# First attention: the keys of a group are loaded with its queries and ahead of them

## The chip, the cores and the metric

The program runs on one core of one Trainium2 chip. The core has TensorE (matmuls, PE in the profile), VectorE (DVE), ScalarE (ACT), GpSimd (POOL) and SyncE (SP), which here does nothing but issue DMAs; the DMAs are carried out by 16 DMA engines of the core. The metric is device time in microseconds of one execution, as a median over runs. The profile is one execution of its own.

## The reference, cut to what matters

`x` and `ctx_2048` have the shape 64 x 64 x 256. Eight blocks follow each other (four pairs of an attention and a feed-forward block), each added to `x`. The change touches the first block alone:

```
def _L0_xattn_ref(q, k, v):            # q = layernorm(x), k = v = ctx_2048
    h = 8
    qh = q.reshape(b * h, d // h, m)   # d = 64: eight channels in each head, m = 256 columns
    kh = k.reshape(b * h, d // h, -1)
    vh = v.reshape(b * h, c // h, -1)
    qk = jnp.einsum('bdm,bdn->bmn', qh, kh) * scale
    sm = jax.nn.softmax(qk, axis=-1)
    return jnp.einsum('bmn,bcn->bcm', sm, vh)
x = x + _L0_xattn_ref(_layernorm(x), ctx_2048, ctx_2048)
```

So there are 64 batches of eight heads, and for each head a 256 x 256 matrix of scores, a softmax over its rows, and a product with the values.

## The kernel before, in words

`first_attention` works through 64 **units** (one batch each, eight heads). A float is split into three bf16 parts, and a score is a product over 72 partitions (nine combinations of parts times eight channels). For that the split parts are stored in DRAM (`z_parts` for the queries, `context_parts` for the keys, lines 185 and 190) and read back spread over partitions: `Q9` (queries, `ratt_Q` in the profile) and `K9` (keys, `ratt_K`). One read serves a **group** of two units, 576 KB of queries (one DMA, line 200) and 576 KB of keys (three DMAs of 192 KB, line 209). There are four buffers of each (`BUFS`), and one semaphore for a buffer, `group_in`, counts the landings of both; TensorE waits for all 64 of a group before the first score of its first unit.

A unit passes twice over TensorE. In slot n, `score(n, h)` (line 419) makes the scores, VectorE takes the maximum of each row of scores (line 591), GpSimd splits these maxima in three bf16 parts (lines 371 to 375), TensorE turns them (`turn_max`, line 428), ScalarE copies the turned row (line 502, semaphore `row_out`), and SP writes it with two small DMAs (`bring_row`, line 216) to three further partitions of `Q9` (semaphore `row_in`). Three slots later (`LAG`), `shift_scores` (line 437) makes the scores again, now with the maxima taken off by those three partitions; it waits for `row_in` at its first head. ScalarE takes the exponential (line 509) and TensorE multiplies with the values (line 461). In the row of PE, score of unit n and shifted score of unit n - 3 take turns, head by head.

The order of each engine is written out by hand: every engine runs a loop over the slot number n, and what stands in one turn of the loop is issued in that order. SP's turn n is, in this order: for n of kind B (below) a load of `x` and of the context (lines 174 and 180); `bring_row(n - 1)`; for odd n `load_q` of the group that starts at unit n + 3; for even n `load_k` of the group that starts at unit n + 2; and then, by n modulo 4, the outputs of four finished units (lines 223, 228, 233, 238 and 240) and the stores of the split parts (lines 185 and 190). SP waits in its order, so `bring_row(n - 1)`, which waits for the row of unit n - 1, holds back all that stands behind it.

In the following a slot is named by n modulo 4: **A** is 0, **B** is 1, **C** is 2 and **D** is 3. Four slots, A to D, are a **period**. The units that open a group are those of A and of C. Before the change, the group that opens at A has its queries issued in SP's turn B and its keys in turn C, and the group that opens at C has its queries issued in turn D and its keys in turn A. SP's turn n begins when the row of unit n - 1 is out, that is late in TensorE's slot n.

`load_q` waits, besides for the stores of `z_parts`, until the last shifted scores of the unit that used the buffer before are written (`written`, four groups earlier). `load_k` had no such wait of its own, as it stood behind `load_q` of the same group.

Of the kernel before, what the change touches and what calls it, by code (L numbers as in the profile page):

```python
# [72 lines left out]
def spread(ap, dim, n):  # L73

    return ap.unsqueeze(dim).to_broadcast(list(ap.shape[:dim]) + [n] + list(ap.shape[dim:]))

def first_attention(nc, io, X, CT, ident, identb, zq, ck, o_dram, r_dram, ST, wsum):
# [3 lines left out]
    BUFS = 4  # L81
# [8 lines left out]
    with ExitStack() as ctx:  # L90
# [21 lines left out]
        veps, rstd, shift = s.sb("veps", [P, 2]), s.sb("rstd", [P, 2]), s.sb("shift", [P, 2, 2])  # L112
# [28 lines left out]
        written, exped, v_in, pv, o_out = (s.sem(x) for x in ("written", "exped", "v_in", "pv", "o_out"))  # L141
# [4 lines left out]
        def is_unit(n):  # L146
            return 0 <= n < UNITS

        def is_pair(a):
            return 0 <= a < PAIRS  # L150

        def at(n, r):

            a, left = divmod(n + LEAD - r, 4)
            return a if left == 0 and is_pair(a) else None

        job, jobs = {}, 0
# [9 lines left out]
        with nc.Block() as block:  # L167

            @block.sync
            def _(sp):  # L170
                def load_x(a):
                    if a > 1:
                        sp.wait_ge(x_in[a % 2], a // 2 * 16)
                    sp.dma_start(X[:, 2 * a:2 * a + 2, :],
                                 x_dram[2 * a:2 * a + 2].rearrange("t p d -> p t d")).then_inc(x_in[a % 2], 16)

                def load_c(a):
                    if a > 1:
                        sp.wait_ge(c_third, a - 1)
                    sp.dma_start(C[:, a % 2],  # L180
                                 c_dram[2 * a:2 * a + 2].rearrange("t p d -> p t d")).then_inc(c_in[a % 2], 16)

                def store_c(a, part):
                    sp.wait_ge((c_first, c_second, c_third)[part], a + 1)
                    sp.dma_start(ck.rearrange("r s a h u m -> s a h r (u m)")[part, a],
                                 CS[:, part].rearrange("p u m -> p (u m)")).then_inc(c_out[part], 16)

                def store_z(a, part):
                    sp.wait_ge((z_first, z_second, z_third)[part], a + 1)
                    sp.dma_start(zq.rearrange("s r a h u m -> s a h r (u m)")[part, a],  # L190
                                 ZS[:, part].rearrange("p u m -> p (u m)")).then_inc(z_out[part], 16)

                def load_q(g):
                    pair, b = g // 2, g % 2
                    for part in range(3):
                        sp.wait_ge(z_out[part], pair * 16 + 16)
                    if g >= BUFS:
                        sp.wait_ge(written, job["shift", 2 * (g - BUFS) + 1, 3] + 1)
                    q = zq.rearrange("s r a (b h) u m -> (s r) a b (h u m)", b=2)[:, pair, b, :]
                    sp.dma_start(Q9[0:R, g % BUFS].rearrange("p h u m -> p (h u m)"), spread(q, 1, 3)).then_inc(  # L200
                        group_in[g % BUFS], 16)

                def load_k(g):
                    pair, b = g // 2, g % 2
                    for part in range(3):
                        sp.wait_ge(c_out[part], pair * 16 + 16)
                    k = ck.rearrange("r s a (b h) u m -> (r s) a b (h u m)", b=2)[:, pair, b, :]
                    for part in range(3):
                        sp.dma_start(K9[24 * part:24 * part + 24, g % BUFS].rearrange("p h u m -> p (h u m)"),
                                     k).then_inc(group_in[g % BUFS], 16)  # L210

                def bring_row(n):
                    u, buf = n % 2, n // 2 % BUFS
                    sp.wait_ge(row_out, n + 1)
                    for c in range(2):
                        sp.dma_start(Q9[R:RM, buf, :, u, c * P:(c + 1) * P],
                                     rows[c * 3 * NH0:(c + 1) * 3 * NH0, u, :]).then_inc(row_in[u], 16)

                def out(a):
                    sp.wait_ge(o_out, a * 4 + 4)  # L220
                    for g in range(4):
                        to = o_dram.rearrange("a (w g) c m -> a g c w m", g=4)[a, g]
                        sp.dma_start(to, O[32 * g:32 * g + DH0 + 1, a % 2].rearrange(
                            "p w u m -> p w (u m)")).then_inc(to_dram[a % 2], 16)

                def sums_back(a):
                    sp.wait_ge(to_dram[a % 2], a // 2 * 64 + 64)
                    sp.dma_start(inv[:, a % 2], o_dram[a][:, DH0, :].rearrange(
                        "w (k m) -> w k m", k=8)).then_inc(d_in[a % 2], 16)

                def inverses_out(a):
                    sp.wait_ge(inverted, a + 1)
                    sp.dma_start(r_dram.rearrange("a w (k m) -> (a w k) m", k=8)[a * P:(a + 1) * P],
                                 inv[:, a % 2]).then_inc(r_out[a % 2], 16)

                def back(a):
                    sp.wait_ge(r_out[a % 2], a // 2 * 16 + 16)
                    sp.dma_start(den[:, a % 2].rearrange("p u m -> p (u m)"), spread(r_dram[a], 1, DH0)).then_inc(
                        o_back[a % 2], 16)
                    sp.dma_start(num[:, a % 2].rearrange("p u m -> p (u m)"), o_dram[a][:, 0:DH0, :]).then_inc(  # L240
                        o_back[a % 2], 16)

                sp.dma_start(decay[:], spread(io["L3_xattn_decay"], 0, P)).then_inc(decay_in, 16)
                for n in range(-LEAD - 3, UNITS + 11):
                    if at(n, -3) is not None:
                        load_x(at(n, -3))
                        load_c(at(n, -3))
                    if is_unit(n - 1):
                        bring_row(n - 1)
                    if n % 2 and is_unit(n + 3):  # L250
                        load_q((n + 3) // 2)
                    if n % 2 == 0 and is_unit(n + 2):
                        load_k((n + 2) // 2)
                    c = n // 4 - 2
                    if n % 4 == 0:
                        if is_pair(c - 1):
                            inverses_out(c - 1)
                        if is_pair(c):
                            out(c)
                    if n % 4 == 1 and is_pair(c):  # L260
                        sums_back(c)
                    if n % 4 == 2 and is_pair(c - 1):
                        back(c - 1)
                    for part in range(3):
                        if at(n, 3 + part) is not None:
                            store_c(at(n, 3 + part), part)
                        if at(n, 6 + part) is not None:
                            store_z(at(n, 6 + part), part)
                    if n == -LEAD + 1:
                        sp.wait_ge(ones_set, 1)  # L270
                        for buf in range(BUFS):
                            sp.dma_start(K9[R:RM, buf].rearrange("p h u m -> p (h u) m"),
                                         spread(ones[:], 1, 2 * NH0)).then_inc(ones_in, 16)
# [3264 lines left out]
```

## Time and profile before

| what | us |
| --- | --- |
| median of 3 runs | 1953.99 (1953.58 to 1956.91) |
| the profiled execution, whole | 1960.88 |
| its span in the trace | 1959.0 |
| first attention: first score to last score | 31.9 to 499.0 |

The span is the time from the first to the last instruction in the trace; about 1.9 us lie around it. The profiled execution took 6.9 us more than the median of the timed runs.
### The profile page before, as it was taken

How to read it: one execution, taken by the hardware profiler on the slowest of the kernel's cores; microseconds unless marked ns; L12 is line 12 of the kernel's file. 1: busy time of each engine (PE TensorE's matmuls, PEld its weight loads, DVE VectorE, ACT ScalarE, POOL GpSimd, SP SyncE). 2: the span in 40 equal slices, each digit the busy share in tenths (PEclk: the TensorE clock that was granted, in tenths of full speed). 3: DMA queues.
4: the chain of work that ended last, by engine and by line, in shares of the span. 5: the costliest groups of instructions: out<-in, count | busy, mean ns of one | idle time of the engine just before them, and what ended most of it. 6: DMA issues, size and time to landing. Idle time of an engine off the chain costs nothing. (4 is left out here: it accounts for less than half of the span.)

```text
span 1959.0 us, 32199 instructions
## 1 busy us (share of the span) xinstructions
PE 1359.7 (69%) x11551; PEld 857.7 (44%) x11572; DVE 1317.5 (67%) x2817; ACT 1105.8 (56%) x1568; POOL 575.1 (29%) x1047
## 2 busy tenths in 40 slices
PE   3989889899469876987435666379999546773111
PEld 1655555555257762555312333246666423442100
DVE  4777677677245534688849999536665567775896
ACT  2767676676412214677537889534444437775554
POOL 6555555553300013111013433201110111112663
PEclk9989898899779997999655667679999768777555
DMA  5565665655310003433010000011111210000111
GB/s 157 130 158 149 143 156 146 165 123 134 78 31 1 0 5 62 78 73 74 9 69 1 1 1 1 22 38 45 30 38 33 91 23 1 1 1 11 44 54 43
DMA packets 96676, 118.46 MB, mean 60 GB/s; under 512 B 29984, under 2 KB 82408, under 8 KB 91916
## 3 DMA queue, kind: packets, MB, share of 16 engines
q1 hardware_dynamic: 96524, 116.46, 24.1%
q8 instruction: 91, 1.49, 0.3%
q14 instruction: 61, 0.50, 0.1%
HBM read 80.07 MB, written 22.88 MB: 53 GB/s over the span
## 5 line engine op out<-in xcount | busy, mean ns | idle before, releaser
L591 DVE TENSOR_REDUCE ratt_nmax<-ratt_psS 128x2 f32<-128x512 f32 x512 | 321.9, 685 | 129.0 <-PE ratt_psS L419 127.4
L509 ACT ACTIVATE ratt_E<-ratt_psT 128x1024 f32<-128x1024 f32 x256 | 256.2, 1023 | 124.6 <-PE ratt_psT L437 124.2
L419 PE MATMUL ratt_psS<-ratt_K,ratt_Q 72*128 72x256 bf16 x1024 | 217.3, 299 | 54.8 <-DMA ratt_K<-context_parts 48.8
L437 PE MATMUL ratt_psT<-ratt_Q,ratt_K 75*128 75x256 bf16 x1024 | 208.5, 289 | 0.6 <-ACT ratt_E L509 0.3
L419 PEld LDWEIGHTS ratt_psS<-ratt_K,ratt_Q 72*128 72x128 bf16 x1024 | 85.7, 103 | 153.5 <-DVE ratt_nmax L591 56.7
L461 PE MATMUL ratt_psO<-ratt_E,ratt_V 128*32 128x256 f32 x2048 | 148.2, 410 | 0.7 <-ACT ratt_E L509 0.7
L437 PEld LDWEIGHTS ratt_psT<-ratt_Q,ratt_K 75*128 75x128 bf16 x1024 | 105.7, 104 | 23.3 <-issue 2.1
L3414 PE MATMUL final_psT<-final_identh,final_Z 128*128 128x128 f16 x64 | 8.3, 311 | 110.4 <-ACT final_Z L3448 110.4
L461 PEld LDWEIGHTS ratt_psO<-ratt_E,ratt_V 128*32 128x32 f32 x2048 | 55.8, 114 | 56.1 <-issue 34.5
L371 POOL TENSOR_TENSOR ratt_parts<-ratt_nmax,ratt_zero 128x16 bf16<-128x16 f32 x64 | 17.1, 268 | 214.5 <-DVE ratt_nmax L591 214.5
L906 ACT COPY sffn_XS<-sffn_psG 128x512 f32<-128x512 f32 x8 | 4.7, 585 | 124.7 <-PE sffn_psG L855 124.7
L2216 PE MATMUL nffn_psH<-nffn_W,nffn_QT 128*128 128x512 bf16 x121 | 52.9, 583 | 30.9 <-ACT nffn_H L2295 20.4
L2409 POOL TENSOR_TENSOR all_X<-all_X,satt_bo 128x1024 f32<-128x1024 f32 x8 | 18.9, 2365 | 167.4 <-DVE all_X L2474 167.4
L2770 DVE SCALAR_TENSOR_TENSOR gffn_H<-gffn_psU,gffn_uwu,gffn_S 128x512 f32<-128x512 f32 x64 | 46.1, 745 | 28.4 <-ACT gffn_S L2945 27.4
L2873 PE MATMUL gffn_psG<-gffn_WG,gffn_QT 128*128 128x512 bf16 x120 | 48.3, 487 | 22.9 <-DVE gffn_H L2770 19.5
L872 PE MATMUL sffn_psH<-sffn_XS,sffn_W 128*128 128x256 f32 x256 | 59.9, 394 | 3.8 <-ACT sffn_XS L906 3.8
L2246 PE MATMUL nffn_psO<-nffn_W,nffn_HT 128*128 128x256 bf16 x256 | 47.5, 348 | 18.7 <-DVE all_X L2135 17.4
L881 PE MATMUL sffn_psO<-sffn_W,sffn_H 128*128 128x256 f32 x256 | 57.4, 383 | 4.4 <-ACT sffn_H L916 4.4
L1282 DVE SCALAR_TENSOR_TENSOR gatt_PB<-gatt_psS,gatt_PB 128x512 f32<-128x512 f32 x64 | 41.2, 686 | 26.0 <-PE gatt_psS L1023 20.8
L3414 PEld LDWEIGHTS final_psT<-final_identh,final_Z 128*128 128x128 f16 x64 | 6.2, 141 | 114.0 <-ACT final_Z L3448 83.1
L872 PEld LDWEIGHTS sffn_psH<-sffn_XS,sffn_W 128*128 128x128 f32 x256 | 49.9, 197 | 12.7 <-issue 3.0
L2587 ACT COPY satt_AT<-satt_psF 128x256 f32<-128x256 f32 x32 | 12.0, 374 | 76.4 <-PE satt_psF L2524 76.4
(474 smaller groups left out, 3693.8 us busy)
## 6 DMA issues: line engine op xcount, KB each, us to landing
ratt_Q<-z_parts SPq DMA_DIRECT2D x32, 576.0 KB
ratt_K<-context_parts SPq DMA_DIRECT2D x96, 192.0 KB
gatt_V<-in_ctx_dram SPq DMA_DIRECT2D x16, 512.0 KB, 6.7
context_parts<-ratt_CS SPq DMA_DIRECT2D x48, 128.0 KB, 5.3
z_parts<-ratt_ZS SPq DMA_DIRECT2D x48, 128.0 KB, 5.5
head_sums<-ratt_O SPq DMA_DIRECT2D x64, 72.0 KB
all_X<-in_x_dram SPq DMA_DIRECT2D x16, 256.0 KB, 3.8
ratt_C<-in_ctx_dram SPq DMA_DIRECT2D x16, 256.0 KB, 3.9
```

Of the source, the lines that this page charges most:

```text
L419: mm = nc.tensor.matmul(psS[:, RING[h], c * D:(c + 1) * D], Q9[0:R, buf, h, n % 2, c * P:(c + 1) * P], K9[0:R, buf, h, n % 2, :], start=Tr ...
L437: mm = nc.tensor.matmul(psT[:, j % 2, e, c, :], K9[0:RM, buf, h, u, c * P:(c + 1) * P], Q9[0:RM, buf, h, u, :], start=True, stop=True)
L461: mm = nc.tensor.matmul(psO[32 * g:32 * g + 32, q, :], V9[:, m % 2, c, q * 4 + g, :], E[:, m % 2 * 2 + q, g, c, :], start=(c == 0), stop=( ...
L509: sc.activation(E[:, m % 2 * 2 + p // 2, 2 * (p % 2):2 * (p % 2) + 2], psT[:, j % 2], ACT.Exp, scale=SCALE).then_inc(exped, 1)
L591: v.tensor_reduce(nmax[:, n % 2, h, :], psS[:, RING[h]].rearrange("p (c t) -> p c t", c=2), AX.X, ALU.max, negate=True).then_inc(maxed, 1)
L872: mm = nc.tensor.matmul(psH[:, f % 2, ff, :], W1[:, k, c * P:(c + 1) * P], XS[:, k, :], start=(k == 0), stop=(k == KC - 1))
L881: mm = nc.tensor.matmul(psO[:, b, :], H[:, c, b * P:(b + 1) * P], W2[:, c, :], start=(c == 0), stop=(c == FC - 1))
L1282: v.scalar_tensor_tensor(half, heads.psS[:, r].rearrange("p (h t) -> p h t", t=L), float(DH) ** -0.5, half, ALU.mult, ALU.mult).then_inc(h ...
L2216: nc.tensor.matmul(psH[:, j % 2, cols], QT[:, g % 2, k, j * P:(j + 1) * P], W1[:, k, cols], start=(k == 0), stop=False)
L2246: mm = nc.tensor.matmul(psO[:, j % 2, 0:D], HT[:, j % 2, n, :], W2[:, n, :], start=(n == 0), stop=(n == FF // P - 1))
L2770: v.scalar_tensor_tensor(H[:, g % 2, j, h * HALF:(h + 1) * HALF], psU[:, h, :], uwu[:, g % 2, j:j + 1], S[:, h, :], ALU.mult, ALU.mult).th ...
L2873: nc.tensor.matmul(psG[:, h, :], QT[:, g % 2, k * G + j, :], WG[:, k, cols], start=(k == 0), stop=(k == KC - 1))
```

## The change

`load_k` moves one slot up: it is issued in the same odd turn as `load_q` of its group, directly in front of it and directly behind `bring_row`. As it now stands ahead of `load_q`, it gets the wait for the buffer's last reader for itself.

```
--- before.py
+++ after.py
@@ -204,6 +204,8 @@
                     pair, b = g // 2, g % 2
                     for part in range(3):
                         sp.wait_ge(c_out[part], pair * 16 + 16)
+                    if g >= BUFS:
+                        sp.wait_ge(written, job["shift", 2 * (g - BUFS) + 1, 3] + 1)
                     k = ck.rearrange("r s a (b h) u m -> (r s) a b (h u m)", b=2)[:, pair, b, :]
                     for part in range(3):
                         sp.dma_start(K9[24 * part:24 * part + 24, g % BUFS].rearrange("p h u m -> p (h u m)"),
@@ -248,9 +250,8 @@
                     if is_unit(n - 1):
                         bring_row(n - 1)
                     if n % 2 and is_unit(n + 3):
+                        load_k((n + 3) // 2)
                         load_q((n + 3) // 2)
-                    if n % 2 == 0 and is_unit(n + 2):
-                        load_k((n + 2) // 2)
                     c = n // 4 - 2
                     if n % 4 == 0:
                         if is_pair(c - 1):
```

No DMA is added or taken away, and no other engine has another instruction; the whole difference is in the order of SP's queue. The first place is SP's turns B and C in the full pipeline, before: from the loads of `x` and context that open turn B, over the row of unit A and the queries of the next A, to the row and the keys that turn C issues.

```order
L174 DMA all_X<-in_x_dram 128x2x256
L180 DMA ratt_C<-in_ctx_dram 128x2x256
L216 DMA ratt_Q<-ratt_rows 3x8x128 x2
L200 DMA ratt_Q<-z_parts 72x1x4096
L228 DMA ratt_inv<-head_sums 128x1x64
L185 DMA context_parts<-ratt_CS 16x8x512
L216 DMA ratt_Q<-ratt_rows 3x8x128 x2
L209 DMA ratt_K<-context_parts 24x4096 x3
```

The same place after (line numbers from 207 on are higher by two):

```order
L174 DMA all_X<-in_x_dram 128x2x256
L180 DMA ratt_C<-in_ctx_dram 128x2x256
L218 DMA ratt_Q<-ratt_rows 3x8x128 x2
L211 DMA ratt_K<-context_parts 24x4096 x3
L200 DMA ratt_Q<-z_parts 72x1x4096
L230 DMA ratt_inv<-head_sums 128x1x64
L185 DMA context_parts<-ratt_CS 16x8x512
L218 DMA ratt_Q<-ratt_rows 3x8x128 x2
```

What moved: the keys that turn C issued (`ratt_K` x3) now stand in turn B, in front of the queries and so also in front of the summaries' load, the context store and the row of unit B.

The second place is SP's turns D and A, before, from the row of unit C to the stores of the finished units:

```order
L216 DMA ratt_Q<-ratt_rows 3x8x128 x2
L200 DMA ratt_Q<-z_parts 72x1x4096
L185 DMA context_parts<-ratt_CS 16x8x512
L190 DMA z_parts<-ratt_ZS 16x8x512
L216 DMA ratt_Q<-ratt_rows 3x8x128 x2
L209 DMA ratt_K<-context_parts 24x4096 x3
L233 DMA inverse_sums<-ratt_inv 128x64
L223 DMA head_sums<-ratt_O 9x4x512 x4
```

And after:

```order
L218 DMA ratt_Q<-ratt_rows 3x8x128 x2
L211 DMA ratt_K<-context_parts 24x4096 x3
L200 DMA ratt_Q<-z_parts 72x1x4096
L185 DMA context_parts<-ratt_CS 16x8x512
L190 DMA z_parts<-ratt_ZS 16x8x512
L218 DMA ratt_Q<-ratt_rows 3x8x128 x2
L235 DMA inverse_sums<-ratt_inv 128x64
L225 DMA head_sums<-ratt_O 9x4x512 x4
```

What moved: the keys that turn A issued stood behind two stores and behind the row of unit D; now they stand in turn D, in front of the queries, and turn A has no large load any more.

## Rows read from the trace of the kernel before

**Rows 1.** The page: span; busy engines; three of the lines in 40 slices of 49 us

```profile
span 1959.0 us, 32199 instructions
...
PE 1359.7 (69%) x11551; PEld 857.7 (44%) x11572; DVE 1317.5 (67%) x2817; ACT 1105.8 (56%) x1568; POOL 575.1 (29%) x1047
...
PEclk9989898899779997999655667679999768777555
DMA  5565665655310003433010000011111210000111
GB/s 157 130 158 149 143 156 146 165 123 134 78 31 1 0 5 62 78 73 74 9 69 1 1 1 1 22 38 45 30 38 33 91 23 1 1 1 11 44 54 43
```

**Rows 2.** Waits of 0 to 700 us: who waited for whom, us, times, longest

```profile
PE ratt_psS L419 <- DMA ratt_K<-context_parts: 48.8, 16, 15.2
...
DVE ratt_nmax L591 <- PE ratt_psS L419: 127.4, 136, 9.7
ACT ratt_E L509 <- PE ratt_psT L437: 124.2, 174, 5.4
```

**Rows 3.** Waits of the steady stretch, 83.25 to 475.57 us

```profile
PE ratt_psS L419 <- DMA ratt_K<-context_parts: 33.2, 14, 3.5
PE ratt_psT L437 <- DMA ratt_Q<-ratt_rows: 0.2, 1, 0.2
```

**Rows 4.** Windows: steady stretch, slots, transfers, an idle stretch; columns in the first line

```profile
core 0: us, PE busy (x) PEld busy (x) DVE busy (x) ACT busy (x) POOL busy (x), PEclk, DMA share, GB/s
83.25:475.57 392.32, 355.68 (x3424) 210.65 (x3425) 284.74 (x485) 274.51 (x370) 196.92 (x460) 0.90 0.61 147
83.25:89.44 6.19, 6.12 (x65) 3.71 (x66) 4.97 (x8) 4.56 (x6) 3.30 (x6) 1.00 0.54 139
171.18:180.16 8.98, 8.95 (x66) 4.85 (x66) 5.29 (x8) 4.70 (x6) 1.11 (x2) 0.65 0.37 107
180.16:186.82 6.66, 6.59 (x73) 4.17 (x69) 5.37 (x10) 6.20 (x10) 4.05 (x8) 1.00 0.52 131
186.82:193.01 6.19, 6.12 (x69) 3.72 (x66) 5.84 (x12) 5.19 (x8) 4.40 (x12) 1.00 0.70 174
193.01:202.29 9.28, 6.19 (x70) 3.71 (x66) 5.62 (x10) 5.32 (x8) 7.11 (x16) 0.95 0.91 187
202.50:205.50 3.00, 3.00 (x16) 2.09 (x14) 2.08 (x4) 1.02 (x1) 0.45 (x1) 0.50 0.83 229
213.00:216.00 3.00, 2.93 (x34) 1.92 (x33) 2.21 (x5) 2.71 (x5) 2.14 (x2) 1.00 0.69 182
237.50:242.50 5.00, 4.93 (x49) 2.98 (x43) 3.06 (x5) 3.62 (x6) 0.99 (x5) 0.86 0.01 1
```

**Rows 5.** Timeline of TensorE: first scores of units 8, 20, 24, 54, 60; the last (start, us, idle before)

```profile
83.25 0.28 PE L419 MATMUL ratt_psS<-ratt_K,ratt_Q 72*128 72x256 bf16 x1 [0.60 <-DMA ratt_K<-context_parts]
...
171.18 0.61 PE L419 MATMUL ratt_psS<-ratt_K,ratt_Q 72*128 72x256 bf16 x2 [2.84 <-DMA ratt_K<-context_parts]
...
202.29 0.39 PE L419 MATMUL ratt_psS<-ratt_K,ratt_Q 72*128 72x256 bf16 x1 [3.02 <-DMA ratt_K<-context_parts]
...
432.46 0.28 PE L419 MATMUL ratt_psS<-ratt_K,ratt_Q 72*128 72x256 bf16 x1 [0.38 <-DMA ratt_K<-context_parts]
...
475.57 0.28 PE L419 MATMUL ratt_psS<-ratt_K,ratt_Q 72*128 72x256 bf16 x1 [0.44 <-DMA ratt_K<-context_parts]
...
498.90 0.28 PE L419 MATMUL ratt_psS<-ratt_K,ratt_Q 72*128 72x256 bf16 x1
```

**Rows 6.** Timeline of SP's queue: DMA issues, start, us for the group

```profile
190.23 0.81 SPq L200 DMA_DIRECT2D ratt_Q<-z_parts  x1
191.09 0.60 SPq L228 DMA_DIRECT2D ratt_inv<-head_sums  x1
191.73 0.60 SPq L185 DMA_DIRECT2D context_parts<-ratt_CS  x1
192.37 1.55 SPq L216 DMA_DIRECT2D ratt_Q<-ratt_rows  x2
194.04 1.20 SPq L209 DMA_DIRECT2D ratt_K<-context_parts  x3
...
210.19 1.56 SPq L216 DMA_DIRECT2D ratt_Q<-ratt_rows  x2
211.87 1.18 SPq L209 DMA_DIRECT2D ratt_K<-context_parts  x3
213.10 0.36 SPq L233 DMA_DIRECT2D inverse_sums<-ratt_inv  x1
213.50 2.83 SPq L223 DMA_DIRECT2D head_sums<-ratt_O  x4
...
220.20 1.56 SPq L216 DMA_DIRECT2D ratt_Q<-ratt_rows  x2
221.92 0.81 SPq L200 DMA_DIRECT2D ratt_Q<-z_parts  x1
```

**Rows 7.** DMA view of 190.2 to 192.4 us: size, us from issue to landing

```profile
context_parts<-ratt_CS SPq DMA_DIRECT2D x1, 128.0 KB, 5.2
ratt_inv<-head_sums SPq DMA_DIRECT2D x1, 32.0 KB, 5.6
```

**Rows 8.** Timeline of ScalarE: the copy of a row in a fast slot

```profile
197.89 0.24 ACT L502 COPY ratt_rows<-ratt_psS 48x128 bf16<-48x128 bf16 x1
```

More of the change, by code:

```diff
@@ L206, in load_k @@
                         sp.wait_ge(c_out[part], pair * 16 + 16)
+                    if g >= BUFS:
+                        sp.wait_ge(written, job["shift", 2 * (g - BUFS) + 1, 3] + 1)
                     k = ck.rearrange("r s a (b h) u m -> (r s) a b (h u m)", b=2)[:, pair, b, :]
@@ L250, in _ @@
                     if n % 2 and is_unit(n + 3):
+                        load_k((n + 3) // 2)
                         load_q((n + 3) // 2)
-                    if n % 2 == 0 and is_unit(n + 2):
-                        load_k((n + 2) // 2)
                     c = n // 4 - 2
```

## The prediction

> **What bounds the kernel now.** I read the page first [rows 1]. No engine fills the span, PE is the busiest with 69%, and in the first quarter, which is the first attention, PE is busy for 0.8 to 0.9 of each slice while the DMA engines carry 123 to 166 GB/s at a share of 0.5 to 0.6. The rest of the program has the same instructions in the same order before and after, so only this stretch counts. Next come its waits [rows 2]. VectorE and ScalarE wait for PE there (127.4 and 124.2 us), and what PE waits for is keys: 48.8 us in 16 waits, the longest, 15.2 us, being the start of the pipeline. In the steady stretch, from the first score of unit 8 to that of unit 60, it is 33.2 us in 14 waits, against 0.2 us for the rows of maxima [rows 3].
>
> Then I looked at single slots [rows 4]. In the period that begins at 171.18 us, slots A to D take 8.98, 6.66, 6.19 and 9.28 us. D is long because PE stands still at its end until the keys of the next A are in: 3.02 us ahead of unit 24, 2.84 us ahead of unit 20 [rows 5]. A is long for another reason. It has no wait of note, but the granted clock is 0.65 in it, while it is 1.00 in B and C: PE, having stood still for 2.84 us, comes back at 1.2 GHz for most of the slot. Slot A of unit 8, which had waited only 0.60 us, ran at 1.00 and took 6.19 us [rows 4, 5]. So one late load costs twice: the wait, and 8.98 - 6.19 = 2.79 us of slow clock behind it.
>
> **The floor.** With every load in time a period is 6.19 + 6.66 + 6.19 + 6.19 = 25.23 us, where D's 6.19 is taken from C, which has the same instructions. The steady stretch is 13 periods in 392.32 us [rows 4], or 30.18 each. 392.32 - 13 x 25.23 = 64.3 us lie above the floor; 33 us of that are waits [rows 3], the other 31 us slow clock.
>
> **The keys of A, from turn C to turn B.** SP issued the queries at 190.23, the keys at 194.04, and unit 24 began when the keys were in, at 202.29 [rows 5, 6]. Between the two issues stand the summaries' load, a context store and the row of unit B, 2.8 us of SP's time. The keys now go at 190.23 and the queries 1.2 us later. How soon both are in has to be bounded. While such a load runs, the DMAs carry 182 to 229 GB/s [rows 4], so 576 KB take 2.6 to 3.2 us. The small load behind the queries, issued at 191.09, was in 5.6 us later, at 196.7, which is 6.5 us behind the queries' issue [rows 6, 7]. With another 576 KB in front of it, it would be 9.1 to 9.7 us behind the first issue, and the queries before it. So by the old timing all is in at 199.6 or so, where PE was free at 202.29 - 3.02 = 199.27. The wait shrinks from 3.0 to about 0.3 us by this alone.
>
> **The keys of C, from turn A to turn D.** They cost PE next to no wait: of the 14 waits one is a C's, 0.38 us ahead of unit 54 [rows 5], and the others are A's. What they did is hold SP. Turn A, from its row to the queries of turn B, took 221.92 - 210.19 = 11.73 us, of which the keys are 1.2 [rows 6]. Now turn A is 10.5 us. The load itself falls into a stretch in which the DMA engines stood still before (share 0.01 from 237.5 to 242.5 us [rows 4]), so it costs nobody anything, as long as that hole stays open.
>
> **The new period, from its own start at 0.** In a fast slot the row is copied 197.89 - 193.01 = 4.9 us after the slot's begin [rows 4, 8], and SP issues it 0.3 us later, at 5.2. Ten and a half us on, at 15.7, SP issues the keys for the next A, at 16.9 the queries. At most 9.7 us behind the first, at 25.4, both and the load behind them are in; PE wants them at 25.23. The queries come before that load, so I count no wait here. Behind them stand the context store and the row of unit B. The context store behind the old queries was issued at 191.73 and in after 5.2 us, 6.7 us behind the queries' issue [rows 6, 7]; with the keys in front this is 9.3 to 9.9, and the row, one place further, comes 0.2 to 0.8 us after it by my estimate (its issue takes 1.55 us, a store's 0.60 [rows 6]). That is 25.2 to 26.4. PE needs this row for the first shifted score, about 0.3 us into the next slot A, at 25.5. So there is a new wait of 0 to 0.9 us in each period, for a row instead of for keys; I take 0.6, above the middle, because turn A's issues now fall on a load in flight. Thirteen of them are 8 us. A pause of 0.60 us left the clock at 1.00 [rows 4, 5], so I charge no slow clock. The row of unit D, behind keys and queries of turn D, is wanted two slots later, and the row of unit A moves forward with turn A; both cost nothing.
>
> **The new wait** for the buffer's last reader stands behind `bring_row(n - 1)`, which waits for a row that PE turns one slot after it has written those shifted scores. It is met when SP comes to it; cost 0. If that were wrong, the queries and rows behind it would be late with it.
>
> **Weighed against a page.** These sentences can be left out. The Trainium skill, "DMA: Bandwidth & Descriptors", section "Queues, rings and completion order", says that each DMA engine takes the descriptors of one issuer's queue in ring order. That speaks against this change, since rows of 12 KB in all then stand behind 1.2 MB. No row here shows a small DMA passing a large one, and the 5.6 us of the 32 KB load [rows 7] agree with the rule. The same page, "Specifications", gives about 27 GiB/s for an engine; all 16 would bring 1.2 MB in 2.6 us, while the rows' 182 to 229 GB/s make it 5.1 to 6.5. By the page there is no new wait and the time is 1953.99 - 64.3 = 1889.7. I go by the rows.
>
> **The sum.** 64.3 - 8 = 56 us less in the stretch, and the start, where the keys of unit 0 can go while SP waited for the queries' stores, is left at 0. A barrier ends the block, so later work moves up by as much. The profiled execution (span 1959.0) would have a span of 1903. The timed median is 6.9 us under the profiled execution, all but 1.9 of it outside of what I can place; I take the gain as the same there: 1953.99 - 56 = 1898 us.
>
> **Rivals.**
> *The queue becomes the bound, half the gain.* In a period of 30.2 us the DMA engines had a hole of some 5 us [rows 4], so their work fills about 25 us, as long as the floor. A share of 0.61 over 392.32 us is 239 us of work, which is 0.73 of 13 x 25.23; a K or Q load runs at 0.69 to 0.83, so there is little left over. For it: SP's issues in turn A already stretch (2.83 us for four stores [rows 6]), and now they fall on keys and queries of turn D still in flight. If that adds 2 to 3.5 us to a period, and part of it brings the slow clock back, 26 to 40 us of 64 go: 1916 to 1930, say 1925. Against it: the loads of a period are spread over its two halves now, and the hole is filled.
> *The wait only moves.* The row of B comes so late that PE stands still for over 2 us at each A, and the slow clock returns in full. Price per period 2.2 + 2.8 = 5, the saving is gone: 1954. For it: the row stands behind twice the bytes. Against it: it had no wait to speak of before, 0.2 us in all [rows 3], and by the sum is late by 0.6.
> *Slower.* The burst of turn D delays the stores of turn A, and so the row of A, wanted at slot D, and the burst of turn B the row of B, wanted at the next A. From the point where both are over 2 us late, two pauses in a period bring two slow slots: 2 x (2.2 + 2.8) = 10, against 4.95 saved; 13 x 5 = 65 us more, 2019. SP would need some 5 us more in turn A than it has had.
> *It does nothing.* SP reaches the keys no sooner, as it waits in turn B for the stores of `z_parts` anyway. Those are waits of `load_q`, behind which nothing of the keys stands now. Time 1954.
>
> **How the numbers follow.** Forecast 0.68, with 1886 to 1912 as its own range (0 to 1.7 us lost in a period, and 3 us at the start and end); queue bound 0.18; wait moves 0.05; nothing 0.03; slower 0.06. The range of 8 in 10 reaches from 1885 into the second case, to 1930. Faster by over 0.2%, which is about what a measurement of this kernel can tell from none: 0.68 + 0.18 + 0.01 = 0.87; same 0.07; slower 0.06.
>
> **What would show it.** Right: slots A at a granted clock of 1.00 and 6.2 us; the clock of the first attention near 1.00 in all slices; PE's waits for `ratt_K` under 5 us behind the start; a few tenths of a us for `ratt_rows` at each A; last score near 443 us instead of 499 [rows 5]; the DMA share in the stretch at 0.7. Wrong: slots A still above 8 us, or waits for `ratt_rows` above 2 us, or an SP turn A that is no shorter than 11 us. The forecast falls if the clock drops without a pause ahead of it, which no slot here shows in the steady stretch.

## The result, and the profile after

| | before | after |
| --- | --- | --- |
| median, us | 1955.45 (4 runs) | 1901.88 (4 runs, 1898.31 to 1904.76) |
| profiled execution, its span | 1960.88, 1959.0 | 1898.31, 1896.4 |
| steady stretch, unit 8 to unit 60 | 392.32 | 329.02 |
| first score to last score | 31.9 to 498.9 | 31.9 to 434.2 |

The ratio is 0.9723, with a 95% interval of 0.9692 to 0.9755. The change makes the kernel 54 us faster; 1898 us were forecast, from the 1953.99 us that were known then.

The page of after. The same lines stand in [rows 1]:

```profile
span 1896.4 us, 32248 instructions
...
PE 1327.3 (70%) x11572; PEld 840.8 (44%) x11572; DVE 1313.4 (69%) x2817; ACT 1104.5 (58%) x1568; POOL 577.0 (30%) x1047
...
PEclk9999999997799959997556667699999678877555
DMA  6577777663100033431200000111110300000111
```

PE has lost 32 us of busy time with the same work in it: its matmuls take half as long where the clock is no longer down. PEclk, which had four 8s among its 9s in the first ten slices, is now 9 (0.9 and more) in all slices of the first attention, and that ends more than a slice earlier.

What PE waits for in the steady stretch, against [rows 3]:

```profile
PE ratt_psS L420 <- DMA ratt_Q<-z_parts: 0.7, 2, 0.5
...
PE ratt_psT L438 <- DMA ratt_Q<-ratt_rows: 0.4, 2, 0.3
```

33.2 us for keys have become 0.7 us for the load that now comes last, the queries, and the rows of maxima cost 0.4 us. Next the windows, against [rows 4]: the stretch, and then the slots A, B, C, D of one period and the next A.

```profile
core 0: us, PE busy (x) PEld busy (x) DVE busy (x) ACT busy (x) POOL busy (x), PEclk, DMA share, GB/s
81.99:411.01 329.02, 324.20 (x3429) 197.73 (x3425) 280.94 (x485) 273.25 (x371) 198.05 (x460) 1.00 0.71 176
183.50:189.69 6.19, 6.12 (x70) 3.72 (x66) 5.02 (x9) 4.69 (x7) 3.79 (x8) 1.00 0.69 173
189.69:196.36 6.67, 6.60 (x74) 4.18 (x70) 5.38 (x10) 6.21 (x10) 3.95 (x8) 1.00 0.65 141
196.36:202.82 6.46, 6.29 (x69) 3.63 (x66) 5.87 (x12) 5.33 (x8) 4.43 (x12) 1.00 0.60 168
202.82:209.11 6.29, 6.19 (x69) 3.71 (x66) 5.16 (x9) 5.30 (x8) 4.38 (x10) 1.00 0.85 213
209.11:215.73 6.62, 6.29 (x65) 3.63 (x66) 5.47 (x9) 4.59 (x7) 3.71 (x8) 1.00 0.79 207
```

A period is 329.02 / 13 = 25.31 us, where it was 30.18 and the floor was put at 25.23. Both slots A have a granted clock of 1.00; 6.19 us is the floor itself, and the second, 6.62, is one of those in which something is late by tenths. The mean hides two kinds of period. Six of the thirteen take 25.22 to 25.25 us, the floor. Five take 25.5 to 25.8 us, 2.0 us above the floor in all. The last two take 24.74 us, because slot B is 6.19 us there instead of 6.67; in the kernel before it is 6.19 in the last period alone. So the stretch lies 1.0 us above 13 x 25.23 only after 1.0 us has been taken off again at its end. The DMA share rises from 0.61 to 0.71 with the same bytes in less time.

SP's queue in two turns A and B of after, from the row to the keys (start, us):

```profile
163.42 1.56 SPq L218 DMA_DIRECT2D ratt_Q<-ratt_rows  x2
165.03 0.42 SPq L235 DMA_DIRECT2D inverse_sums<-ratt_inv  x1
165.50 2.69 SPq L225 DMA_DIRECT2D head_sums<-ratt_O  x4
...
171.63 1.58 SPq L218 DMA_DIRECT2D ratt_Q<-ratt_rows  x2
173.38 2.17 SPq L211 DMA_DIRECT2D ratt_K<-context_parts  x3
...
188.65 1.57 SPq L218 DMA_DIRECT2D ratt_Q<-ratt_rows  x2
...
200.25 1.15 SPq L211 DMA_DIRECT2D ratt_K<-context_parts  x3
201.56 0.83 SPq L200 DMA_DIRECT2D ratt_Q<-z_parts  x1
```

Turn A with its row takes 9.96 us to the next large load in the first and 11.60 in the second, where it took 11.73 in [rows 6]. The mean of the thirteen is 10.0 us, beside 11.3 before; only one, the 11.60, is above 11, the sign of being wrong that the prediction named. The load starts earlier than before, and the queries stand directly behind it.

The row of unit B is now a tight place. In this period the keys are issued at 225.60, and the first shifted score of the next slot A has to wait for that row:

```profile
225.60 1.15 SPq L211 DMA_DIRECT2D ratt_K<-context_parts  x3
...
234.77 0.39 PE L420 MATMUL ratt_psS<-ratt_K,ratt_Q 72*128 72x256 bf16 x2
235.33 0.39 PE L438 MATMUL ratt_psT<-ratt_Q,ratt_K 75*128 75x256 bf16 x2 [0.16 <-DMA ratt_Q<-ratt_rows]
```

The row is in 235.33 - 225.60 = 9.7 us after the keys' issue, a wait of 0.16 us. The last score starts 64.7 us sooner than that in [rows 5]:

```profile
434.21 0.39 PE L420 MATMUL ratt_psS<-ratt_K,ratt_Q 72*128 72x256 bf16 x2
```

### The profile page after: what moved, and what is told of

It is laid out like the page before. It is cut to its first block and busy times, and to the rows that moved or that the text cites. A ratio compares the mean times of both kernels' runs of the same rounds, so it can differ in the third digit from the quotient of the medians.

```text
span 1896.4 us, 32248 instructions
## 1 busy us (share of the span) xinstructions
PE 1327.3 (70%) x11572; PEld 840.8 (44%) x11572; DVE 1313.4 (69%) x2817; ACT 1104.5 (58%) x1568; POOL 577.0 (30%) x1047
## 5 line engine op out<-in xcount | busy, mean ns | idle before, releaser
L592 DVE TENSOR_REDUCE ratt_nmax<-ratt_psS 128x2 f32<-128x512 f32 x512 | 318.0, 682 | 65.4 <-PE ratt_psS L420 65.0
L420 PE MATMUL ratt_psS<-ratt_K,ratt_Q 72*128 72x256 bf16 x1024 | 203.6, 283 | 22.1 <-DMA ratt_Q<-z_parts 15.9
L438 PE MATMUL ratt_psT<-ratt_Q,ratt_K 75*128 75x256 bf16 x1024 | 195.5, 274 | 0.8 <-DMA ratt_Q<-ratt_rows 0.4
L462 PE MATMUL ratt_psO<-ratt_E,ratt_V 128*32 128x256 f32 x2048 | 137.9, 387 | 0.7 <-ACT ratt_E L510 0.7
L420 PEld LDWEIGHTS ratt_psS<-ratt_K,ratt_Q 72*128 72x128 bf16 x1024 | 80.7, 99 | 112.9 <-DVE ratt_nmax L592 62.5
L438 PEld LDWEIGHTS ratt_psT<-ratt_Q,ratt_K 75*128 75x128 bf16 x1024 | 99.6, 98 | 18.0 <-issue 2.1
L462 PEld LDWEIGHTS ratt_psO<-ratt_E,ratt_V 128*32 128x32 f32 x2048 | 53.6, 109 | 50.5 <-issue 27.2
```

What stands on the lines that cost most here:

```text
L420: mm = nc.tensor.matmul(psS[:, RING[h], c * D:(c + 1) * D], Q9[0:R, buf, h, n % 2, c * P:(c + 1) * P], K9[0:R, buf, h, n % 2, :], start=Tr ...
L438: mm = nc.tensor.matmul(psT[:, j % 2, e, c, :], K9[0:RM, buf, h, u, c * P:(c + 1) * P], Q9[0:RM, buf, h, u, :], start=True, stop=True)
L462: mm = nc.tensor.matmul(psO[32 * g:32 * g + 32, q, :], V9[:, m % 2, c, q * 4 + g, :], E[:, m % 2 * 2 + q, g, c, :], start=(c == 0), stop=( ...
L592: v.tensor_reduce(nmax[:, n % 2, h, :], psS[:, RING[h]].rearrange("p (c t) -> p c t", c=2), AX.X, ALU.max, negate=True).then_inc(maxed, 1)
```

## The experiments

### Each half of the move alone

`a_keys_only` moves only the keys of the groups that open at A, from turn C to turn B:

```
                     if n % 2 and is_unit(n + 3):
-                        load_k((n + 3) // 2)
+                        if (n + 3) // 2 % 2 == 0:
+                            load_k((n + 3) // 2)
                         load_q((n + 3) // 2)
+                    if n % 2 == 0 and is_unit(n + 2) and (n + 2) // 2 % 2 == 1:
+                        load_k((n + 2) // 2)
```

`c_keys_only` has the two remainders the other way round (`== 1` above, `== 0` below): only the keys of the groups that open at C move, from turn A to turn D.

> Only half of the move: the keys of the groups that open at slot A go from turn C to turn B ahead of the queries; those that open at C stay in turn A. My theory: the late load is cured, but SP's turn A keeps its 1.2 us of key issues and the DMA engines keep their hole, so loads come 1.2 to 2 us later than in the changed kernel, which had only tenths to spare. Waits of 1 to 2 us at most slots A, some with the slow clock behind them: 1915 to 1935 us, most of the gain is there. The rival, that the relief of turn A is what made the loads early, expects under a third of the gain: above 1937 us.

Measured: 1914.99 us, ratio 0.983 (0.9792 to 0.9869), at the lower end of what was expected; the rival's "under a third of the gain" is out. The stretch, two slots A, and the first scores that open these two, with the pause ahead of them:

```profile
81.24:430.44 349.20, 334.60 (x3428) 200.88 (x3425) 282.46 (x485) 273.36 (x371) 197.36 (x460) 0.97 0.66 166
160.26:167.69 7.43, 7.43 (x65) 4.41 (x66) 5.56 (x9) 4.48 (x6) 2.85 (x5) 0.77 0.49 125
241.50:250.45 8.95, 8.94 (x65) 4.87 (x66) 5.80 (x9) 4.69 (x6) 2.64 (x3) 0.65 0.42 110
...
160.26 0.39 PE L423 MATMUL ratt_psS<-ratt_K,ratt_Q 72*128 72x256 bf16 x2 [1.08 <-DMA ratt_Q<-z_parts]
...
241.50 0.39 PE L423 MATMUL ratt_psS<-ratt_K,ratt_Q 72*128 72x256 bf16 x1 [2.28 <-DMA ratt_Q<-z_parts]
```

349.20 us are 26.86 a period. A pause of 1.08 us was followed by a slot of 7.43 us at 0.77, one of 2.28 us by 8.95 us at 0.65. Waits of 1 to 2 us at most slots A were expected; of the thirteen from unit 12 on, four came after 1.06 to 2.28 us, one after 0.98, and the others after less or none.

> The other half: the keys of the groups that open at slot C go from turn A to turn D; those that open at A stay in turn C, where they wait behind the row of unit B. My theory: these keys are still issued about 7.2 us into slot C and land some 8 us later, so TensorE waits 2 to 3 us at each slot A as before and the slow clock follows: 1945 to 1954 us, periods of 29.5 to 30.2 us. The rival (relief of turn A is the cause) expects 1902 to 1920 us.

Measured: 1918.10 us, ratio 0.9842 (0.9797 to 0.9887), and here my expectation was wrong. The stretch, its waits, and one load, issue by issue, to the score that it lets go:

```profile
85.85:438.89 353.04, 335.98 (x3424) 202.43 (x3425) 282.03 (x485) 273.89 (x370) 197.22 (x458) 0.96 0.70 163
PE ratt_psS L423 <- DMA ratt_K<-context_parts: 14.5, 12, 3.1
...
180.64 0.83 SPq L200 DMA_DIRECT2D ratt_Q<-z_parts  x1
...
184.94 1.15 SPq L211 DMA_DIRECT2D ratt_K<-context_parts  x3
...
190.93 0.28 PE L423 MATMUL ratt_psS<-ratt_K,ratt_Q 72*128 72x256 bf16 x1 [0.43 <-DMA ratt_K<-context_parts]
```

A period is 27.16 us, and the time lies in the range of the rival, 1902 to 1920. The keys of A are still issued in turn C, but they are in after 190.93 - 184.94 = 6.0 us, not after 8.25 as in [rows 5, 6]. I had carried the 8.25 us over as if they were a property of the load. They were not, and 8.25 was near the top even before: from unit 12 to unit 56 the keys' issue was 6.8 to 8.3 us ahead of the first score of A. In `c_keys_only` it is 5.6 to 6.1 us in seven of these twelve, 7.1 to 7.5 in the other five.

With the keys of C gone from turn A, SP comes to the queries of the next A sooner: they are issued 4.3 us ahead of the keys, where it was 3.8, and 2.6 us into slot C (which opens at 178.06) instead of 3.4. In the kernel before, the distance from queries to keys is 3.8 or 3.9 us at each of these A. In `c_keys_only` it is 4.2 to 5.4 us wherever the keys are in within 6.2 us, and 3.9 in four of the five slow ones (4.4 in the fifth). So the queries are further on when the keys come. That this is what lets the keys through sooner is my inference: the two go together, no run moved one of them alone, and `c_keys_only` also took 576 KB out of turn A, which may count by itself.

So the rival has its share: the relief of turn A alone brings periods from 30.18 to 27.16, the earlier slot alone to 26.86, both together to 25.31. The parts give 3.0 and 3.3 us and the whole 4.9, since each takes from the same loss, and once it is gone there is nothing left to take. Alone, neither is enough: `c_keys_only` still waits 14.5 us in 12 waits, the longest 3.1 us.

### Which of the two loads goes first

```
-                        load_k((n + 3) // 2)
                         load_q((n + 3) // 2)
+                        load_k((n + 3) // 2)
```

> The changed kernel with the two loads of a group swapped: queries first, keys directly behind them, same slot. TensorE waits for both on one count, so by my theory only the slot matters and not the order in it: the time of the changed kernel, 1902 us, within 4. The rival, that the keys have to stand ahead of the queries, expects the waits of slot A back in part: 1915 to 1954 us.

> The changed kernel once more, on the chip and beside the kernels of this call, since the chips of the calls differ: 1895 to 1905 us, ratio to the kernel before 0.970 to 0.976. If keys first and queries first (1912.8 us, last score at 445.9 us against 434.3) only differed by chip, this comes out near 1912.

Measured: queries first 1912.81 us, ratio 0.9826 (0.9787 to 0.9865). The changed kernel again 1896.14 us, ratio 0.9711 (0.9674 to 0.9748), last score at 433.7. The two intervals of the ratio do not meet, so the order matters by itself, and "only the slot matters" was wrong. The 1912.81 us fell between what I expected (1898 to 1906) and what the rival did (1915 to 1954). The stretch and the waits with queries first:

```profile
84.62:422.57 337.95, 328.59 (x3428) 198.63 (x3425) 281.54 (x485) 273.19 (x371) 198.12 (x460) 0.99 0.71 171
PE ratt_psS L420 <- DMA ratt_K<-context_parts: 3.9, 4, 1.2
PE ratt_psT L438 <- DMA ratt_Q<-ratt_rows: 1.7, 4, 0.6
```

26.00 us a period, against 25.31; one of the thirteen slots A fell to 0.64 of the clock and took 9.37 us, behind a pause of 1.24 us. The DMA views from the first issue of the pair show where it begins; each number is a tenth of a microsecond. Keys first (changed kernel, from 200.25):

```profile
GB/s 67 15 0 0 13 46 3 0 0 410 246 82 0 0 164 164 246 328 164 410 246 328 246 164 164 164 82 82 82 410 82 164 82 164 82 492 0 164 164 164
```

Queries first (from 203.08):

```profile
GB/s 287 328 231 159 120 141 108 92 92 92 174 51 21 10 10 338 174 246 82 82 164 0 82 0 164 0 328 328 164 328 164 328 410 246 0 328 164 246 246 82
```

With keys first the large load begins to flow in the tenth slice, 0.9 us behind its issue (the 410); with queries first in the sixteenth, 1.5 us behind (the 338; what is in front of it is the end of earlier stores). The one DMA of 576 KB takes 0.8 us to issue and starts 0.6 us later than the first of three DMAs of 192 KB, issued in 0.4 us each. This is no accident of one period. Keys and queries move in packets of 8 KB. In 24 of the 26 groups from unit 8 to unit 58 of the changed kernel the first such packet starts 0.92 to 0.95 us behind the keys' issue, and in 25 of the 26 with queries first it starts 1.57 to 1.61 us behind the queries' issue, whether earlier DMAs are still running or not. When the queries go second, that delay lies behind the keys' transfer. In a stretch in which the row of B had only tenths to spare, 0.6 us in front of it is enough to be felt. Why the larger DMA starts later is open: it differs in size and in its number of partitions (72 against 24).

### The loads ahead of the row

```
+                    if n % 2 and is_unit(n + 3):
+                        load_k((n + 3) // 2)
+                        load_q((n + 3) // 2)
                     if is_unit(n - 1):
                         bring_row(n - 1)
-                    if n % 2 and is_unit(n + 3):
-                        load_k((n + 3) // 2)
-                        load_q((n + 3) // 2)
```

> The changed kernel with the loads of the group ahead of the row of maxima in the same turn of SP, in place of behind it. If a DMA engine serves the queue in order, the rows of A and C land behind 1.2 MB: some 9 us after the loads' issue instead of 2.8 us after their own. The row of A, out 5 us into slot B, is wanted at the begin of slot D, 12.9 us after B's; it is then 2 to 4 us late in each period, with the slow clock behind it: period 28 to 31 us, 1930 to 1965 us. The rival, that a small DMA passes the large ones (or that where the row stands is of no account), expects the changed kernel's time.

Measured: 1998.25 us, ratio 1.0234 (1.0182 to 1.0285): slower than the kernel before by 1.8 to 2.9%, and slower than I expected (1930 to 1965). The waits of the steady stretch, three slots B, C and D of a period, and the row of unit A from its issue to the shifted score that it lets go:

```profile
PE ratt_psT L438 <- DMA ratt_Q<-ratt_rows: 56.8, 13, 5.6
...
192.97:199.64 6.67, 6.60 (x73) 4.18 (x70) 5.37 (x10) 6.21 (x10) 4.06 (x8) 1.00 0.42 67
199.64:205.83 6.19, 6.12 (x70) 3.72 (x66) 5.84 (x12) 5.20 (x8) 4.42 (x12) 1.00 0.81 207
205.83:219.54 13.71, 9.16 (x70) 5.00 (x66) 5.89 (x10) 5.14 (x8) 4.20 (x9) 0.75 0.83 184
...
202.74 1.53 SPq L218 DMA_DIRECT2D ratt_Q<-ratt_rows  x2
...
210.78 0.61 PE L438 MATMUL ratt_psT<-ratt_Q,ratt_K 75*128 75x256 bf16 x2 [4.55 <-DMA ratt_Q<-ratt_rows]
```

The row (6 KB in each of two DMAs) is in 8.0 us after its issue, behind keys and queries. It is 4.55 us late for slot D, the clock goes down, and D takes 13.71 us in place of 6.19. The 13 waits are 4.4 us each in the mean, where 2 to 4 were expected, and all 13 slots D have a clock of 0.57 to 0.75 and take 11.3 to 15.9 us. A period is 33.2 us (28 to 31 expected). That the loads stand behind the row and not ahead of it is therefore worth 102 us (1998.25 against 1896.14, same chip): the same DMAs in the same turn of SP.

### What the slow clock costs by itself

The kernel before, with 24 matmuls that serve nothing in front of the wait for keys at each A from unit 12 on:

```
+                    if h == 0 and n > 1:
+                        pe.wait_ge(row_out, n - 1)
+                    if h == 0 and n % 4 == 0 and n >= 12:
+                        for f in range(FILL):                      # FILL = 24
+                            nc.tensor.matmul(psS[:, 0, f % 2 * D:(f % 2 + 1) * D], ...)
                     if h == 0 and n % 2 == 0:
                         pe.wait_ge(group_in[buf], n // 8 * GROUP_IN + GROUP_IN)
-                    if h == 0 and n > 1:
-                        pe.wait_ge(row_out, n - 1)
```

The wait for `row_out` only moves from behind the wait for keys to in front of the added matmuls, which write where the row was.

> The kernel before, with 24 matmuls of no use (results overwritten by the first score) put in front of TensorE's wait for keys at each slot A from unit 12 on; TensorE is busy for 2.6 us of the 3 us in which it stood still. The keys come as late as before. My theory splits the loss in halves, the wait and the slow clock behind it: with the pause filled the clock stays at 1.00, slots A take 6.2 us instead of 8.9, and the time falls by 12 x 2.75 = 33 us or somewhat less, as slot A is late for the loads again: 1920 to 1935 us. The rival, that slot A is slow through something else (the load that it shares the memories with, or its own waits), expects no change, 1954 us.

Measured: 1935.92 us, ratio 0.993 (0.9906 to 0.9954). A slot D that ends in the added matmuls, the slot A behind it, and the added matmuls themselves:

```profile
187.03:195.84 8.81, 8.74 (x93) 6.06 (x90) 5.61 (x10) 5.31 (x8) 6.64 (x16) 1.00 0.84 219
195.84:202.02 6.18, 6.11 (x67) 3.70 (x65) 4.97 (x8) 4.56 (x6) 1.40 (x2) 1.00 0.52 143
193.21 2.79 PE L414 MATMUL ratt_psS<-ratt_K,ratt_Q 72*128 72x256 bf16 x24
195.84 0.38 PE L425 MATMUL ratt_psS<-ratt_K,ratt_Q 72*128 72x256 bf16 x2
...
281.56 0.39 PE L425 MATMUL ratt_psS<-ratt_K,ratt_Q 72*128 72x256 bf16 x2 [1.35 <-DMA ratt_K<-context_parts]
```

The keys are about as late as before: where a wait is left behind the added matmuls, they are in 7.3 to 8.5 us after their issue, against 6.8 to 8.3 in the kernel before. D is nearly as long (8.81 us), and A is back at 6.18 us with a clock of 1.00. So it is in eleven of the twelve slots A of the stretch that have added matmuls ahead of them. The one that is not, behind the last line above, still had a pause of 1.35 us after the added matmuls, and it took 7.69 us at 0.78. So the slow clock follows from the pause and from nothing else in slot A.

The stretch falls from 392.32 to 367.28 us, by 25 of the 64 us above the floor. What the slots A take above 6.19 us falls by more, from 30.6 us to 1.4 (the one slot), which is the clock's share as the prediction had it. The difference is the filling's own price: 13 x 2.6 us of matmuls and 3.1 us of waits behind them stand where 32.6 us of waits for A had been. The medians show 13 us (1935.92 beside 1948.76 for the kernel before on the same chip), where I had expected 33 or somewhat less and a time up to 1935: by the timed runs this was a miss, if a narrow one in the time.

### The start

The changed kernel with 150 small matmuls in the 15 us ahead of unit 0 and five behind each score of units 0 to 2.

```
+                        for f in range(150):
+                            warm()     # nc.tensor.matmul(psO[:, 0, 0:P], identb[:], identb[:], ...)
...
                                 score(n, 2 * p + e)
+                                if n < 3:
+                                    for f in range(5):
+                                        warm()
```

> The changed kernel with matmuls of no use (their result is never read) at the start: 150 in the 15 us in which TensorE waits for the first keys and queries, and 5 behind each score of units 0 to 2. In the changed kernel slot 3 takes 8.94 us at 1.2 GHz, as TensorE had stood half idle in slots 0 to 2. If the clock follows what TensorE did just before, slot 3 comes down to about 6.2 us and units 1 to 3 are no slower: 3 to 4 us less by the trace, last score near 431 us, which the medians may not tell from none. If slot 3 is slow for another reason, nothing, or a loss of 1 to 5 us where the added matmuls stand in the way.

Measured: 1897.45 us, beside 1896.14 for the changed kernel on the same chip: no difference in the medians, which the expectation allowed for. Slot 3 of the changed kernel, with a pair of its matmuls, first:

```profile
47.82:56.76 8.94, 8.94 (x50) 5.39 (x49) 6.69 (x11) 4.24 (x5) 5.38 (x14) 1.00 0.29 80
50.38 0.64 PE L420 MATMUL ratt_psS<-ratt_K,ratt_Q 72*128 72x256 bf16 x2
```

Then, with the added matmuls: the 150, the first score, and slots 0 and 3.

```profile
16.27 10.35 PE L426 MATMUL ratt_psO<-all_identb 128*128 128x128 bf16 x150
34.09 0.61 PE L420 MATMUL ratt_psS<-ratt_K,ratt_Q 72*128 72x256 bf16 x2 [7.48 <-DMA ratt_Q<-z_parts]
...
34.09:41.17 7.08, 7.08 (x56) 6.18 (x57) 4.81 (x8) 0.00 (x0) 2.38 (x2) 0.55 0.79 200
51.64:58.05 6.41, 5.65 (x52) 3.14 (x50) 6.00 (x11) 4.11 (x5) 4.53 (x10) 1.00 0.42 113
```

Slot 3 came down from 8.94 to 6.41 us as expected, but the keys and queries of unit 0 were in 2.2 us later (34.09 against 31.91), PE had stood still for 7.48 us by then, and slot 0, full of slow added matmuls, took 7.08 us where it had taken 4.76. The last score was at 435.9, where I had expected some 431. In the other ten traces of this document the first score starts at 30.6 to 32.4 us; whether the added matmuls made it later here is not shown. So the slow slot at the start can be had back, but not with this filling; at most 2.5 us are there, and I left it. Slot 3 of the changed kernel also shows a trap: its granted clock reads 1.00, while a pair of matmuls takes 0.64 us as at half clock [rows 5]. The trace's record of the clock begins only at 56.8 us there, so the durations decide.

### How much the kernel before varies

> The kernel before once more, for a second trace. By the traces so far the first attention alone gives 64.7 us (last score 499.0 against 434.3 and 433.9), while the medians of two calls differ by 53.6 and 56.8 us. If the first attention varies from run to run in the kernel before, its last score here is well under 499 (near 492); if the rest of the program varies, the last score is at 499 again and the 1459.9 us behind it differ.

> A third trace of the kernel before, for the same question: last score near 499 with a rest that varies by some us, or a last score that varies.

| trace | last score, us | span behind it, us |
| --- | --- | --- |
| before | 498.9 | 1460 |
| before_again | 493.8 | 1460 |
| before_third | 498.6 | 1463 |
| after | 434.2 | 1462 |
| after_again | 433.7 | 1456 |

Both vary: the first attention of the kernel before by 5 us, the untouched rest by 7. By the traces the first attention gives 60 to 65 us. The medians gave 54 and 57 (with an interval of some 6 us to either side). For the first pair the difference can be placed: last score 64.7 us sooner, rest 2.1 us longer, so 62.6 us between the two profiled executions. The one of before was 5.4 us above its median (1960.88 beside 1955.45), the one of after 3.6 below (1898.31 beside 1901.88), and 62.6 - 5.4 - 3.6 = 53.6. Why executions of one kernel differ by that much stays open.

## Why the prediction was right, point by point

**The floor** was 25.23 us a period; 25.31 was measured in the mean, 25.22 to 25.25 in six of thirteen periods. (The highest slice of [rows 1] in the first attention is 165 GB/s, not 166 as I read it; nothing rests on that.) In those six, A and D cost 6.19 us, as C does, as was forecast for a period with nothing late. That B costs 6.67 did not hold at the end of the stretch, where it was 6.19; this made the two last periods 0.5 us shorter than the floor.

**The wait and the clock behind it.** Slot A at 6.2 us and a clock of 1.00 was forecast and seen. That a wait costs twice is shown by filling it. The split, 33 us of waits and 31 us of clock, was borne out in the trace: with the pauses filled, slots A lost 1.4 us where they had lost 30.6. "2.79 us of slow clock" behind a wait was one slot, however. The twelve from unit 12 to unit 56 lost 1.35 to 2.97 us each, and not in the order of the waits: 2.92 us of wait was followed by 7.54 us at 0.77, and 1.88 us by 9.04 at 0.64.

**The keys of A.** That one slot sooner takes most of the wait away held, also alone: of 33.2 us in 14 waits, 8.2 us in 8 were left, for the queries, and 0.2 for keys. But the argument gave the two halves the wrong weights: I left the keys of C no part but 1.2 us of SP's time, and alone they are worth 3.0 us of the 4.9 a period, nearly as much as the keys of A with 3.3. The step that failed was that they "cost PE next to no wait". They were not waited for, but with them in turn A the keys of A were in later; by my inference because they held SP up ahead of the queries. The "0.3 us" that was to be left at A by the earlier slot alone was too little as well: in `a_keys_only` the mean over thirteen A is 0.63 us, up to 2.28.

**The new wait** for the row of B is the term that was mis-sized: 8 us forecast in the stretch, and 0.4 us measured in two waits, with 0.7 us in two more for the queries, where I had counted none. All that is late by tenths, waits or not, came to 2.0 us in five periods. Its parts were nearly right: keys 9.7 us ahead of the row's landing (9.5 to 10.7 forecast), turn A at 10.0 us in the mean (10.5). But a row that lands a few tenths before it is wanted leaves no wait at all, and I took a value above the middle. In `q_first`, with 0.6 us more, waits of the forecast kind do appear (1.7 us for rows and 3.9 us for keys, and the slots longer).

**The sum.** The first attention gained 64.7 us by the traces, not 56: 63.3 in the steady stretch, 1.3 ahead of it, where the prediction had put nothing, and 0.1 behind. That is why the last score came at 434 and not near 443. The timed runs gained 54, which is 11 less than the traces show. The two errors are of opposite sign, and it is partly luck that the median came out within 4 us of the forecast. The step "I take the gain as the same there", from the profiled pair to the timed runs, was not safe to a few microseconds.

**The rivals.** The queue did not become the bound: a share of 0.71 in the stretch left room. The "slower" rival, rows late by more than 2 us and a slow clock behind, can be made to happen, though with one pause in a period and not two: the loads ahead of the row gave 1998 us, where the rival's estimate was 2019. The buffer's own wait cost nothing that the traces show.

## What to carry to other kernels

A load that was 2.5 us late in the mean cost nearly 5 us here, as the slot behind it ran in part at half clock; look at slots, with their clock, before adding up waits. When a load is late, look also at what stands in front of it in the issuing engine's order: a load that nobody waits for can be the reason. And put the small DMAs with a near deadline in front of the large ones: the same loads in front of two 6 KB rows turned a gain of 57 us into a loss of 45, on the same chip.

## What the runs showed of the hardware

- A pause of 0.60 us left TensorE at full clock (unit 8 [rows 5]), one of 1.08 us was followed by a slot at 0.77 and one of 2.28 us by one at 0.65. The length of the pause alone does not tell: in `a_keys_only` 0.98 us was followed by 0.79 and 1.06 us by 1.00, and in `before_third` 1.94 us by 1.00. With the pause filled by matmuls the slot stayed at 1.00.
- The same 576 KB began to flow 0.9 us after the issue as three DMAs of 24 partitions and 1.6 us after it as one of 72 (by the first packet, in nearly every group of two traces).
- Two DMAs of 6 KB behind 1.2 MB in one queue were in 8.0 us after their issue. The Trainium skill's page "DMA: Bandwidth & Descriptors", section "Queues, rings and completion order", has each engine consume its queue in order; this trace agrees.
